# Softmax row sums on GpSimd: one instruction of 1024 columns for both heads in place of two of 512

## What is computed

```python
x = L0_attn_y
xn = _layernorm(x, axis=-1)
x = x + _L0_attn_ref(xn, ...) + _L0_ffn_ref(xn, ...)
# attention, for each of 16 heads and 8 batches:
att = jnp.einsum('bhqd,bhkd->bhqk', q, k) * scale
att = jax.nn.softmax(att, axis=-1)
out = jnp.einsum('bhqk,bhkd->bhqd', att, v)
```

## Time and profile before

| | us |
|---|---|
| median of 3 runs | 3653.11 (3651.51 to 3653.34) |
| the profiled execution | 3649.46 |
| its span, first to last instruction | 3647.7 |
| TensorE busy | 3527.4 (97%) |
| GpSimd busy | 2711.4 (74%) |
| VectorE busy | 2534.3 (69%) |
| ScalarE busy | 1686.6 (46%) |

### The profile page before, as it was taken

One profiled execution on the slowest core, in us unless ns is written; L12 is line 12 of the kernel. 1 busy time (PEld: TensorE's weight loads), 2 busy tenths in 40 slices (PEclk: granted clock), 3 DMA queues, 4 the chain that ended last, 5 costly groups with the idle time before them and its releaser, 6 DMA issues. The chain is left out here.

```text
span 3647.7 us, 59807 instructions
## 1 busy us (share of the span) xinstructions
PE 3527.4 (97%) x16231; PEld 2094.8 (57%) x16232; DVE 2534.3 (69%) x3254; ACT 1686.6 (46%) x3126; POOL 2711.4 (74%) x2322
## 2 busy tenths in 40 slices
PE   7999569999999999999999999999999999999899
PEld 5777445555555555555555555555555555555487
DVE  7888657777777777777777777777777777777444
ACT  4444324444444444444444444444444444444443
POOL 1111138888888888888888888888888888889611
PEclk9999779999999999999999999999999999999899
DMA  7766455666666666666666666666666666664386
GB/s 217 218 200 208 155 125 125 160 171 171 171 171 171 171 171 171 171 171 171 171 171 171 171 171 171 171 171 171 171 171 171 171 171 171 171 171 125 118 313 228
DMA packets 393627, 635.53 MB, mean 174 GB/s; under 512 B 48048, under 2 KB 214640, under 8 KB 393584
## 3 DMA queue, kind: packets, MB, share of 16 engines
q1 hardware_dynamic: 370800, 603.54, 59.4%
q0 software_dynamic: 14336, 23.08, 3.0%
q10 hardware_dynamic: 8448, 8.39, 0.6%
HBM read 306.91 MB, written 126.12 MB: 119 GB/s over the span
## 5 line engine op out<-in xcount | busy, mean ns | idle before, releaser
L1089 DVE TENSOR_REDUCE merged<-psum 128x1 f32<-128x1024 f32 x1024 | 1206.2, 1220 | 731.0 <-PE psum L917 729.2
L1052 ACT ACTIVATE probs<-psum 128x512 f32<-128x512 f32 x2048 | 1083.6, 600 | 1159.5 <-PE psum L891 744.4
L1216 POOL TENSOR_TENSOR sums<-sums,probs 128x512 f32<-128x512 f32 x768 | 981.0, 1277 | 94.9 <-ACT probs L1052 40.2
L1217 POOL TENSOR_TENSOR sums<-sums,probs 128x512 f32<-128x512 f32 x768 | 982.4, 1279 | 0.0
L932 PE MATMUL psum<-probs,v_sb 128*64 128x512 f32 x4096 | 930.2, 596 | 0.0
L888 PE MATMUL psum<-q_full,k_full 128*128 128x512 f32 x2048 | 877.3, 428 | 0.0
L891 PE MATMUL psum<-q_rest,k_rest 65*128 65x512 f32 x2048 | 812.5, 397 | 0.0
L932 PEld LDWEIGHTS psum<-probs,v_sb 128*64 128x64 f32 x4096 | 283.7, 137 | 559.2 <-issue 496.1
L888 PEld LDWEIGHTS psum<-q_full,k_full 128*128 128x128 f32 x2048 | 388.5, 190 | 196.6 <-issue 95.3
L1117 DVE RECIPROCAL sum_all<-sum_all 128x128 f32<-128x128 f32 x512 | 448.8, 918 | 28.3 <-ACT sum_all L1060 28.3
L964 PE MATMUL psum<-x_t,w_qk 128*128 128x512 f32 x1536 | 411.9, 404 | 38.0 <-DVE w_d L1082 27.5
(11 more groups left out here) (143 smaller groups left out, 3085.2 us busy)
## 6 DMA issues: line engine op xcount, KB each, us to landing
x_t<-xt SPq DMA_DIRECT2D x118, 1024.0 KB
k_full<-high SPq DMA_DIRECT2D x256, 256.0 KB
v<-values SPq DMA_DIRECT2D x64, 512.0 KB, 3.2
w_qk<-wqk_parts SPq DMA_DIRECT2D x64, 512.0 KB, 4.0
q_full<-high SPq DMA_DIRECT2D x128, 256.0 KB
q_full<-low SPq DMA_DIRECT2D x128, 256.0 KB
k_rest<-low SPq DMA_DIRECT2D x128, 256.0 KB
q_rest<-high SPq DMA_DIRECT2D x128, 256.0 KB
```

The lines of the kernel that those rows point to most:

```text
L1052: nc.scalar.activation(probs[:, kt, h, :], ring[ring_place(g, j) % RING], ACT.Exp, scale=SCALE).then_inc(probs_ready, 1)
L1089: nc.vector.tensor_reduce(out=merged[:, col:col + 1], in_=work[:, 2 * h:2 * h + 2, :].rearrange("p b c -> p (b c)"), axis=AX, op=ALU.max, ...
L1216: nc.gpsimd.tensor_tensor(sums[:, half, 0, :], first[:, 0, :], probs[:, kt, 0, :], ALU.add)
L1217: nc.gpsimd.tensor_tensor(sums[:, half, 1, :], first[:, 1, :], probs[:, kt, 1, :], ALU.add).then_inc(sums_added, 1)
```

## The change

The two additions of a key tile become one instruction over both heads. `sums[:, half]` and `probs[:, kt]` lie head behind head in memory, so it reads and writes 1024 columns in a row. The waits ahead of it and the semaphore behind it stay as they are; `sums_added` still counts one for each key tile.

```diff
                     else:
                         first = sums[:, half, :, :]
                         pool.wait_ge(sums_added, 14 * s + 7 * half + kt - 1)
-                    nc.gpsimd.tensor_tensor(sums[:, half, 0, :], first[:, 0, :], probs[:, kt, 0, :], ALU.add)
-                    nc.gpsimd.tensor_tensor(sums[:, half, 1, :], first[:, 1, :], probs[:, kt, 1, :], ALU.add
+                    nc.gpsimd.tensor_tensor(sums[:, half, :, :], first, probs[:, kt, :, :], ALU.add
                                             ).then_inc(sums_added, 1)
                 if half == 0 and nxt:
                     fetch(s, par)
```

## The result

The changed kernel takes 3710.93 us (median of 4 runs, 3708.53 to 3713.04), the one before in the same session 3653.23 us (median of 4, 3651.51 to 3653.65): ratio 1.0159, interval 1.0141 to 1.0176. It is slower by 58 us. The profiled execution's span grew from 3647.7 to 3708.6 us, by 60.9.

A forecast was written before the change was run, and what follows sets the result against it. TensorE was taken to bound the loop and GpSimd the tail. Profiled 3649.46 + 69.4 for collisions - 4 for the tail = 3714.9; with the median 3.65 us above the profiled run, 3718 us, range 3680 to 3742.

The forecast's parts named there:

- Who bounds the loop: In the loop TensorE sets the pace and GpSimd has about 11% to spare, so shorter adds bring nothing there.
- The 413 us of ScalarE: ScalarE's recorded 413.4 us wait for GpSimd's adds misleads; at slot 2 it really waits for the scores.
- Length of the joint add: GpSimd's joint add of 1024 columns takes 2.40 us, bounds 2.37 to 2.52, against 2.52 for a pair.
- Where it falls: Half 0, key tile 7: the joint add starts 0.04 us before VectorE's TOKEN0 and shuts it out, each step or none.
- The price of a collision: Before slot 2's projection TensorE stalls 1.12 us a step, in 62 steps: 69.4 us.
- The tail: From 3321.67 us to the last add GpSimd sets the pace; shorter adds gain 4 us, from 0 to 5.
- Sum: Whole kernel: 3649.46 + 69.4 - 4 = 3714.9 us profiled; 3718 us for the median.
- The other signs: Changed profile: line 1143 at 2.4 to 2.5 us, TensorE idle 1.0 to 1.2 us before the projection, step 46.7 us.
- (a): Rival: tile 7's add starts after TOKEN0, no collision, only the tail counts: 3649 us; chance 0.15.
- (b): Rival: collision in some steps only, one of the loop body's two: 3684 us, between 3660 and 3700; chance 0.07.
- (c): Rival: ScalarE's 413 us wait at slot 2 is real, each step gains 0.5 us: 3617 us; chance 0.02.

The follow-up runs named there:

- e6: The changed kernel with the add of key tile 6 of half 0 alone in two instructions: 3649.95 us against 3650.33 for the kernel before, ratio 0.9997.
- e5: The kernel before with joint adds in the last two steps alone (28 of 896): 3647.04 us against 3650.33, ratio 0.9990.
- e2: The changed kernel with one small GpSimd add more ahead of key tile 7 of half 0: 3646.92 us against 3650.48 for the kernel before, ratio 0.9991.
- e7: The kernel before with the add of key tile 7 of half 0 alone joint: 3651.73 us against 3650.33, ratio 1.0003.
- e4: The changed kernel with the three TOKEN instructions moved ahead of the reductions of quad 2: 3648.88 us against 3650.48 for the kernel before, ratio 0.9993.
- e8: The changed kernel with TOKEN0 and TOKEN1 in one accumulating VectorE instruction: 3645.75 us against 3650.33 for the kernel before, ratio 0.9984.
- e1: The kernel before, adds in pairs, with one VectorE reduction more behind TOKEN2 in every step: 3709.54 us against 3650.48, ratio 1.0162.

## Why the prediction was right, point by point

- **Who bounds the loop.** Right. 129 us less work of GpSimd brought nothing there.
- **The 413 us of ScalarE.** The reading as a misattribution holds. In the changed kernel that row shrank to 183.6 us while the one that blames the scores grew from 744.4 to 974.0 us. The waits are the same (ScalarE's idle time before line 1052 is 1159.5 us before and 1159.2 after), and only the instant at which an add happens to end has moved. The waits of ScalarE in the kernel before, then in the changed one:

```profile
ACT probs L1052 <- PE psum L891: 744.4, 172, 6.4
...
ACT probs L1052 <- PE psum L891: 974.0, 228, 6.4
ACT probs L1052 <- POOL sums L1216: 183.6, 36, 5.1
```

- **Length of the joint add.** I took 2.40 us from the rows elsewhere, it was 2.37, the lower bound.
- **Where it falls.** 0.04 us before TOKEN0 was forecast, 0.08 to 0.12 us measured, and in all 62 steps. The prediction had 0.07 us in hand, perhaps 0.25, before TOKEN0 would win. With e6's point of decision at +0.04 us it was 0.12 to 0.16. SILU0 stayed clear of the adds, as forecast: 0.28 to 0.29 us in 62 of its 64 executions.
- **The price of a collision.** This is the term that was mis-sized: 1.12 us a step forecast, 1.00 measured, 69 against 62 us. The reductions were forecast 1.15 us late and are 1.04 in step 33: the add ended 0.07 us sooner, and they follow TOKEN0's end 0.04 us sooner. There was slack after all: the weight load that followed the reduction by 0.06 us and the matmul by another 0.13 now start together, so TensorE starts 0.90 us late. Against that, the second matmul of the projection follows 0.10 us later than before, which I hadn't counted. So two errors partly cancel.
- **The tail.** -4 forecast, -3.4 in the profile, and -3.3 by e5's times. One sign was wrong: of TensorE's waits for GpSimd there the one at line 989 got shorter (2.4 to 0.7 us) but the one at line 942 longer (3.3 to 4.2). A sum of waits in a stretch (5.7 us before, 4.9 after) doesn't tell what the stretch can gain.
- **Sum.** 3649.46 + 62.1 - 3.4 = 3708.2 for the profiled execution; it took 2.2 us more, in stages that the change doesn't touch. 3718 was forecast for the median, 3710.9 measured, at the lower end of the sum's own bounds (3710 to 3736). Part of the distance is the 3.65 us by which the median lay above the profiled execution: in the changed kernel it lies 0.6 above, so that term was no property of the kernel.
- **The other signs.** All are there, and each a little smaller than written: the mean of the new line is 2.37 us (2.39 to 2.41 written), line 1143 takes 2.33 to 2.37 in 62 steps (2.4 to 2.5), TensorE's matmuls are idle for 0.75 us before the projection (1.0 to 1.2), and a step takes 46.64 us (46.7). GpSimd's fetch waits for TOKEN2.
- **The rivals.** (a) No collision: line 1143 rules it out for the changed kernel. What its time would have been, e2 and e7 show, with the order changed. (b) A collision in some steps exists as well, in e6's profile. (c) The 413 us gave nothing: no step got shorter with joint adds, with or without the collision.

## What to carry to other kernels

Before an instruction is made longer on an engine with time to spare, look for who is shut out while it runs, and compare the two starts, not the shares of busy time; a loop whose phases repeat can hit in every step, as here in 62 of 62. Where such a meeting can't be avoided, move the short instruction to where its engine has idle time for the wait and nothing waits closely for what follows (e4), or give it a form that the long one doesn't hold up (e8), rather than rely on a start a few hundredths of a microsecond apart (e6).

## What the runs showed of the hardware that I had not expected

- The joint add that accumulates in place takes 2.36 us in the median, less than the 2.39 to 2.40 us of the two other adds of 1024 columns.
- The order between the two engines is not that of the recorded starts, but it is decided very sharply: adds that start up to 0.038 us after TOKEN0 go first, and from 0.038 us on they go second (e6; the other traces fit).
- The loser's loss isn't symmetric. TOKEN0 waits up to 2.2 us. The add, when it comes second, is longer by 0.06 to 0.10 us only (e6, e7, e1, and step 62 of the kernel before), though TOKEN0 then still has up to 0.24 us of its recorded 0.28 to run; and an add that starts 0.15 to 0.22 us after TOKEN0 isn't longer at all (1.27 us in the kernel before, 2.36 to 2.38 in e7).
- A stall of TensorE ahead of the projection costs 0.10 us more than the stall itself: the second matmul of line 964 follows the first by 0.34 us after a stall and by 0.23 without one, in the changed kernel, e1 and e6 alike. Why, no trace shows.
